# A drain behind each group of matmuls carries TensorE's increment in a graph-attention kernel

## The reference

```python
q, k, v = (feat @ W.T + b).reshape(n, H, HD)              # for Wq, Wk, Wv
score = einsum('ehd,ehd->eh', q[edge_dst], k[edge_src])   # one per edge and head
score = clip(score / sqrt(HD), -10, 10)
alpha = softmax of score over the edges of one destination
wv = segment_sum(alpha * v[edge_src], edge_dst)
x1 = feat + wv @ Wp.T + bp
h = gelu(layernorm(x1) @ W1.T + b1) @ W2.T + b2            # 256 -> 1024 -> 256
out = layernorm(x + x1 + h)
```

## Time and profile before

| | |
|---|---|
| median of 3 runs | 1532.16 us (1528.4 to 1550.74) |
| profiled execution, its own time | 1529.23 us |
| its span, first to last instruction | 1527.4 us |
| mean granted TensorE clock | 0.850 |
| instructions | 25002 |

### The profile page before, as it was taken

How to read it: one execution, slowest core, us unless ns; L and a number is a source line. 1 busy time by engine, 2 the same in 40 slices (tenths; PEclk the granted TensorE clock), 3 DMA queues, 4 the chain that set the end, 5 groups by cost and what they waited for, 6 DMA issues and landing times.

```text
span 1527.4 us, 25002 instructions
## 1 busy us (share of the span) xinstructions
PE 1155.0 (76%) x6166; PEld 702.7 (46%) x6166; DVE 948.5 (62%) x1542; ACT 661.5 (43%) x1906; POOL 750.8 (49%) x800
## 2 busy tenths in 40 slices
PE   8946758768778588777678778677877876878887
PEld 6812325435444344444445444344444444545466
DVE  6816665666656565666666567576576665665673
ACT  2212225345445345345445435444545444534543
POOL 3664554545645544544555555545455545554300
PEclk9966868988978888979889888889788788898799
DMA  9975765655756656666666666756666656666510
GB/s 296 356 232 161 225 208 177 212 172 180 227 157 187 205 173 192 192 183 192 207 181 195 209 177 204 217 166 205 203 184 203 196 168 200 196 201 182 167 52 23
DMA packets 155028, 292.71 MB, mean 192 GB/s; under 512 B 32215, under 2 KB 92469, under 8 KB 154934
## 3 DMA queue, kind: packets, MB, share of 16 engines
q0 software_dynamic: 61536, 200.85, 43.6%
q1 hardware_dynamic: 93398, 90.90, 19.1%
HBM read 257.31 MB, written 34.34 MB: 191 GB/s over the span
## 4 chain that ended last, share of the span: by engine, by line
PE 32%; another core or an unknown queue 25%; issue 18%; DVE 18%; ACT 5%; DVEq 1%; ACTq 0%; DMA 0%; SPq 0%
DVE score L1571 7%; DVE ev L1584 6%; PE bank L475 5%; PE quad L834 4%; PE bank L455 4%; PE quad L895 4%; PE bank L904 4%; PE bank L427 2%; PE bank L917 2%; DVE prod L1564 2%; PE bank L930 1%; PE bank L884 1%; PE bank L421 1%; PE quad L455 1%
## 5 line engine op out<-in xcount | busy, mean ns | idle before, releaser
L394 POOL DMA_INDIRECT kv<-kv_rows,src_sb x750 | 713.7, 952 | 652.1 <-issue 326.4
L1564 DVE TENSOR_TENSOR prod<-kv,quad 128x1024 f32<-128x1024 f32 x196 | 239.3, 1221 | 426.3 <-remote 324.5
L904 PE MATMUL bank<-ev,onehot 128*32 128x264 f32 x1568 | 151.8, 451 | 160.7 <-ACT acc_sb L1174 101.4
L455 PE MATMUL bank<-hT,w_sb 128*128 128x256 f32 x736 | 219.2, 450 | 41.2 <-ACT hid L463 30.0
L1584 DVE TENSOR_TENSOR ev<-kv,bank 128x1024 f32<-128x1024 f32 x196 | 238.0, 1214 | 0.5 <-ACT ev L1160 0.5
L1571 DVE TENSOR_REDUCE score<-prod 128x32 f32<-128x1024 f32 x196 | 237.7, 1213 | 0.8
L895 PE MATMUL quad<-qwin,onehotT 32*128 32x256 f32 x1568 | 158.3, 476 | 79.1 <-issue 40.1
L455 PEld LDWEIGHTS bank<-hT,w_sb 128*128 128x128 f32 x736 | 162.8, 227 | 89.8 <-issue 45.4
L475 PE MATMUL bank<-w_sb,hid 128*128 128x256 f32 x736 | 190.9, 412 | 2.0 <-issue 2.0
L475 PEld LDWEIGHTS bank<-w_sb,hid 128*128 128x128 f32 x736 | 149.5, 208 | 32.0 <-issue 9.7
L1174 ACT ACTIVATE acc_sb<-bank 128x264 f32<-128x264 f32 x98 | 38.1, 389 | 290.7 <-remote 219.8
(11 more groups left out here) (148 smaller groups left out, 1297.7 us busy)
## 6 DMA issues: line engine op xcount, KB each, us to landing
dst_rows<-edge_dstT SPq DMA_DIRECT2D x50, 256.0 KB
qwin<-q_rows SPq DMA_DIRECT2D x392, 32.0 KB
kv_rows<-kv_out SPq DMA_DIRECT2D x24, 512.0 KB
kv<-kv_rows,src_sb POOLq DMA_INDIRECT x750
agg_rows<-acc_sb SPq DMA_DIRECT2D x98, 82.5 KB
xT_sb<-xT SPq DMA_DIRECT2D x25, 256.0 KB
xq_sb<-xT SPq DMA_DIRECT2D x25, 256.0 KB
agg_in<-agg_rows SPq DMA_DIRECT2D x24, 264.0 KB
```

Of the source, the lines that this page charges most:

```text
L394: return nc.gpsimd.indirect_dma_start(out=rows, out_offset=None, in_=kv_dram, in_offset=bass.IndirectOffsetOnAxis(ap=index, axis=0))
L455: last = nc.tensor.matmul(bank[:, j * SB:(j + 1) * SB], w1_sb[:, k * HIDDEN + f * P:k * HIDDEN + (f + 1) * P], hT[:, k], start=(k == 0), s ...
L904: last = nc.tensor.matmul(bank4[WIN * i:WIN * (i + 1), 0:ACC], onehot[:, slot // 2, TILES * (slot % 2) + i, :], ev[:, slot % 4, i], start= ...
L1564: nc.vector.tensor_tensor(prod[:, slot % 2].rearrange("p (i c) -> p i c", c=C), kv[:, slot, :, 0:C], quad[:, :, 0:C], ALU.mult).then_inc(s ...
```

## The change

At eleven places of TensorE's program (`merge`, `q_rows`, `sums`, `project_q`, `transpose_x`, `project_x`, `transpose_wv`, `project_out`, `transpose_h`, `ffn1`, and the last part of `ffn2`) the last matmul no longer increments the group's semaphore. A drain instruction follows it and carries the increment. The waits of the other engines and their counts are as before. The head, the last superblocks' FFN matmuls and the general path, which is not taken here, are unchanged.

```diff
@@ -881,8 +881,8 @@
             def merge(p, slot):
                 pe.wait_ge(s_stc, p + 1)
                 pe.wait_ge(s_csel, p + 1)
-                nc.tensor.matmul(bank4[:, 0:ACC], place[:, slot % 2], staged[:, slot % 2], start=True, stop=True)\
-                    .then_inc(s_mrg, 1)
+                nc.tensor.matmul(bank4[:, 0:ACC], place[:, slot % 2], staged[:, slot % 2], start=True, stop=True)
+                nc.tensor.drain().then_inc(s_mrg, 1)
 
             def q_rows(n, slot, p, uses):
                 pe.wait_ge(s_qwin[slot // 2], 64 * uses)
@@ -892,20 +892,20 @@
                 cols = slice(slot % 2 * P, (slot % 2 + 1) * P)
                 for i in range(TILES):
                     rows = slice(WIN * i, WIN * (i + 1))
-                    last = nc.tensor.matmul(quad[:, i, 0:C], onehotT[rows, slot // 2, cols], qwin[rows, slot // 2],
+                    nc.tensor.matmul(quad[:, i, 0:C], onehotT[rows, slot // 2, cols], qwin[rows, slot // 2],
                                             start=True, stop=True)
-                last.then_inc(s_qe, 1)
+                nc.tensor.drain().then_inc(s_qe, 1)
 
             def sums(n, slot, p):
                 pe.wait_ge(s_ev, n + 1)
                 if slot % 2 == 0 and exists(p - 1, PAIRS):
                     pe.wait_ge(s_accc, p)
                 for i in range(TILES):
-                    last = nc.tensor.matmul(bank4[WIN * i:WIN * (i + 1), 0:ACC],
-                                            onehot[:, slot // 2, TILES * (slot % 2) + i, :], ev[:, slot % 4, i],
-                                            start=(slot % 2 == 0 and (i > 0 or not exists(p - 1, PAIRS))),
-                                            stop=(slot % 2 == 1), skip_group_check=(i == 0))
-                last.then_inc(s_part, 1)
+                    nc.tensor.matmul(bank4[WIN * i:WIN * (i + 1), 0:ACC],
+                                     onehot[:, slot // 2, TILES * (slot % 2) + i, :], ev[:, slot % 4, i],
+                                     start=(slot % 2 == 0 and (i > 0 or not exists(p - 1, PAIRS))),
+                                     stop=(slot % 2 == 1), skip_group_check=(i == 0))
+                nc.tensor.drain().then_inc(s_part, 1)
...
@@ -971,7 +974,8 @@
                     pe.wait_ge(s_w1, 32)
                 if pair > 0:
                     pe.wait_ge(f_ev, 4 * s + pair)
-                ffn1_pair(pair).then_inc(f_f1, 1)
+                ffn1_pair(pair)
+                nc.tensor.drain().then_inc(f_f1, 1)
 
             def ffn2(s, part):
                 if part == 0 and isinstance(s, int) and s == 0:
@@ -982,9 +986,9 @@
                         pe.wait_ge(f_x2, s + 2)
                     else:
                         pe.wait_ge(f_z, s)
-                last = ffn2_part(F2_PARTS[part])
+                ffn2_part(F2_PARTS[part])
                 if part == 2:
-                    last.then_inc(f_f2, 1)
+                    nc.tensor.drain().then_inc(f_f2, 1)
 
             def edges(turn, r, parity):
                 for i in range(SLOTS):
```

The other places have the same form:

```diff
-                wv_transposes().then_inc(f_wvT, 1)
+                wv_transposes()
+                nc.tensor.drain().then_inc(f_wvT, 1)
```

More of the change, by code:

```diff
@@ L916, in project_q @@
                     for k in range(KC):
-                        last = nc.tensor.matmul(bank6[:, a * C:(a + 1) * C], xq_sb[:, k, a * P:(a + 1) * P],
-                                                wqkv_in[:, k, 0:C], start=False, stop=(k == KC - 1))
-                last.then_inc(f_qm, 1)
+                        nc.tensor.matmul(bank6[:, a * C:(a + 1) * C], xq_sb[:, k, a * P:(a + 1) * P],
+                                         wqkv_in[:, k, 0:C], start=False, stop=(k == KC - 1))
+                nc.tensor.drain().then_inc(f_qm, 1)
             def transpose_x(k, rows, bank=bank7, col=0):
                 for j in range(KC):
-                    last = nc.tensor.transpose(bank[:, col + j * P:col + (j + 1) * P], rows[:, j * P:(j + 1) * P], ident[:])
-                last.then_inc(s_xgT, 1)
+                    nc.tensor.transpose(bank[:, col + j * P:col + (j + 1) * P], rows[:, j * P:(j + 1) * P], ident[:])
+                nc.tensor.drain().then_inc(s_xgT, 1)
             def project_x(k, columns, bank=bank7):
@@ L929, in project_x @@
                 for j in range(KC):
-                    last = nc.tensor.matmul(bank[:], columns[:, j], wqkv_in[:, j, C:3 * C], start=False,
-                                            stop=(j == KC - 1))
-                last.then_inc(s_xkvm, 1)
+                    nc.tensor.matmul(bank[:], columns[:, j], wqkv_in[:, j, C:3 * C], start=False,
+                                     stop=(j == KC - 1))
+                nc.tensor.drain().then_inc(s_xkvm, 1)
             def first_x_tiles():
@@ L959, in project_out @@
                     pe.wait_ge(s_wp, 16)
-                out_projection().then_inc(f_y, 1)
+                out_projection()
+                nc.tensor.drain().then_inc(f_y, 1)
             def transpose_h(s):
@@ L965, in transpose_h @@
                     pe.wait_ge(f_ev, 4 * s)
-                h_transposes().then_inc(f_hTp, 1)
+                h_transposes()
+                nc.tensor.drain().then_inc(f_hTp, 1)
             def ffn1(s, pair):
```

## The result

The changed kernel takes 1811.27 us (1806.68 to 1825.15, 4 runs), the kernel before 1538.38 (1528.4 to 1550.74, 4 runs) beside it: ratio 1.1784, 95% interval 1.1667 to 1.1901. That is 18% slower, outside the range of 1215 to 1605. The profiled execution has a span of 1809.3 us, 282 more than before.

A forecast was written before the change was run, and what follows sets the result against it. The prediction took late TensorE increments during dense gather traffic as the bound: 1529.2 us, minus 388 for the unnamed waits, plus 191 for 765 drains, gives 1332, stated as 1330 us, with a range of 1215 to 1605.

The forecast's parts named there:

- What bounds the kernel now: Loop: TensorE's increments arrive up to 8.2 us late while gather traffic is dense; 25% of the chain, 388 us.
- the whole unnamed part of the chain goes: At the eleven places, the drain's increment avoids the held-back route, so 388 us of waits in the chain go.
- the lower end zero: Lower bound of the gain in the chain: nothing, if the drain's notice is as late as the matmul's.
- rival 1: Drains behind TensorE's groups are held too and stop TensorE: 1764 us, bounds 1630 and 1890; chance 0.20.
- two groups released at once: `q_rows` and `merge` end 4 us apart, consumers start 0.12 us apart: taken as completed work with notices held back.
- The term of the drains: 765 drains on TensorE's queue at 0.25 us each, all on the path: 191 us added, ends 0 and 306.
- Released by TensorE within a microsecond: Sign of success in the profile after: `copy_sums` and `products` get TensorE's release within a microsecond.
- DMA's share: Sign of success: the DMA engines' busy share rises to over 0.7.
- The fall of the unnamed share: Sign of success: the chain's "another core or an unknown queue" falls from 25% to some 5%.

The follow-up runs named there:

- D: Series on one chip, kernel before 1516.58 us: no gathers after the first turn, 1081.37 us; the same with the change's drains, 1296.95; the change itself, 1756.34.
- B: Series on another chip, kernel before 1091.63 us: gathers given extra waits, 1091.51, with drains 1271.06; no gathers after the first turn, 1056.82, with drains 1275.17.
- series A: Kernel before (1518.87 us) with bare drains, increments left on matmuls: 1754.46; changed kernel with second drains: 1789.75; gathers of 16 floats: 1527.18, with the change 1763.88.
- series E: Kernel before (1525.29 us) with four memsets, each with a GpSimd drain, after every second gather: 2628.69, with the change 2628.58; GpSimd drain behind every gather instead: 3345.22.

## Why the prediction was wrong

**What bounds the kernel now: right, with one half of its reason wrong.** The 388 us were waits for late TensorE groups, and they are worth about that: 435 us without the gathers in D, of which 35 are the gathers' own by B. But I called them held-back notices of completed work, and tied them to "the gathers' traffic". A wait for TensorE to be idle is as late as the notice, and small rows left them as they were; the stream of gathers makes them, not the bytes.

**The step that failed: that the drain's "increment takes a route that is not held back", so that "the whole unnamed part of the chain goes", 388 us.** No part of the wait went, only its name. The drain returned as late as the increment had, and it stopped TensorE for that time. I had written the alternative down (the lower end zero, and rival 1) and gave it 0.20, on the strength of two groups released at once. Those rows show only that one cause held both; TensorE "had gone on issuing" in them because nothing had asked it whether it was idle. They did not speak against rival 1 at all. The rule of the Trainium skill ("PSUM — Partial Sum Buffer", section "Engine vs sequencer instructions"), that a drain waits until the engine is fully idle, put the drain no earlier than the matmul's increment. The traces agree: 5.5 us from the end of `sums` to `stage` in after, and no drain before the matmul's increment where both are recorded (series A).

**The term of the drains: right.** 0.25 us for each was taken; 0.235 (B) and 0.28 (B and D, without gathers) were measured where nothing is held. There all of it lay on the path, as assumed, with TensorE the busiest engine; in series E, where GpSimd is the bound, none of it did. How much of it is on the path of the change itself no run separates from the held drains.

**Rival 1: right in kind, 47 us short.** It had 72 stalls of 1.5 to 2.4 us, 140 us in all, and half of the drains' 191. There were some 125 held stretches of some 280 us. Not all of these are new: TensorE stood idle behind late notices before too, and its idle time grew by 144 us in all. The other 140 are busy time. Drains alone add 60 to 76 us to it in B and D, where the clock stays near full: a group begins behind the modelled end of the one before, and no longer beside it. So some 64 to 80 us, an estimate, are left for the lower clock, for which rival 1 had no term. That its total comes within 3% is in part luck. No run separates the clock from the waits that lower it.

**The signs to look for.** "Released by TensorE within a microsecond" failed, and so did DMA's share (0.54 where over 0.7 was asked). The fall of the unnamed share to nothing came, though I had it as a sign of success; rival 1 had it growing. A wait behind an instruction that the profile knows is named, however long it is.

**Settled and open.** Shown: the cost is the drain's wait, not its increment; its bare price; that gathers make TensorE's completions late, not by their bytes; that the drain is late with them. Not settled: why the chip of series B shows no lateness with all gathers in one streak (each chip was seen in one series only), what in a gather holds a TensorE completion, and whether the streak or the mean rate decides. For the streak speaks that 27 gathers in a row hold a drain for 18.75 us in the changed kernel and later, shorter streaks for 7.3 at most. For a kernel that is faster than both, on the chips where releases are late, gathers would have to be issued without holding TensorE; no run here found a way.

## What to carry to other kernels

A drain asks whether the engine is idle, so it can't be earlier than the completion of the last matmul, and it stops the queue until then: put it behind nothing whose successors could run, and count 0.24 to 0.28 us for each wherever the engine sets the pace. When a notice is late, ask first whether the notice or the completion is, and look for a row in which something already waits for the engine to be idle; two consumers released together don't tell. When a share of the chain disappears, look whether the idle time of the waiting engines went too.

## What the runs showed of the hardware

- One unchanged kernel takes 1092 us in one series and 1517 to 1538 in five others. In the latter's traces with gathers in a row TensorE's completions come late, by up to 8 us in the rows shown and by 18.75 us behind a streak of 27. TensorE's clock is 0.98 in the first and 0.85 in the trace of before; with the gathers gone it is 0.975 in one of the others (D) too.
- A gather's record ends after 0.95 us and the next can start 1.25 us after its start, but with a drain on GpSimd behind it the next comes 3.2 us after its end: 3345 us for the kernel.
- A drain on TensorE ends 0.03 us after the increment of the last matmul in 92 of 122 cases in which both are late. A second drain right behind the first ends 0.07 us after it.
